# Macaron block (MoE, attention, MoE) on one core: the columns of 14 groups of normalised rows come from DMA transposes instead of TensorE

## The reference

```python
x = x + 0.5 * moe(layernorm(x))      # 4096 tokens of width 256
x = x + attention(layernorm(x))      # 4 sequences of 1024, 16 query heads, 4 key/value heads, RoPE
x = x + 0.5 * moe(layernorm(x))
# moe: softmax router over 32 experts, top 8 kept up to a share of 0.8; every expert is
# computed for every token: silu(x @ gate) * (x @ up) @ down, weighed per token
```

## Time and profile before

| | |
|---|---|
| median of 3 runs | 2312.97 us (2312.69 to 2313.44) |
| the profiled execution | 2313.61 us |
| its span in the profile | 2311.8 us |
| PE busy | 2240.8 us (97%) |
| DVE / ACT / POOL busy | 1581.2 / 1242.3 / 1063.5 us |
| PE in the chain that ended last | 90% |

### The profile page before, as it was taken

The page is one execution under the profiler, slowest core; times in us unless marked ns, Lnnn a source line. Parts: engine busy times, 40 slices in busy tenths (PEclk is TensorE's granted clock), DMA queues, the critical chain, the costliest instruction groups (busy, mean ns, idle before and its releaser), DMA issues.

```text
span 2311.8 us, 48013 instructions
## 1 busy us (share of the span) xinstructions
PE 2240.8 (97%) x19280; PEld 1498.7 (65%) x19280; DVE 1581.2 (68%) x3138; ACT 1242.3 (54%) x1973; POOL 1063.5 (46%) x864
## 2 busy tenths in 40 slices
PE   2999999999999999999999999999999999999998
PEld 2888875555565565565556555665655655688887
DVE  7766579877877877877777876676777753454543
ACT  4433331666666666566666566666656666533332
POOL 1866653443443443443434434333433434465665
PEclk9999999999999999999999999999999999999999
DMA  5210121011101011100110111010010010011010
GB/s 214 74 39 24 39 57 30 17 28 31 30 17 50 20 37 25 30 23 20 44 30 22 25 32 31 11 41 14 19 42 11 15 36 10 21 29 30 19 39 19
DMA packets 111878, 77.78 MB, mean 34 GB/s; under 512 B 57508, under 2 KB 103844, under 8 KB 110888
## 3 DMA queue, kind: packets, MB, share of 16 engines
q1 hardware_dynamic: 111512, 74.69, 11.7%
q10 hardware_dynamic: 144, 0.03, 0.0%
HBM read 62.87 MB, written 11.80 MB: 32 GB/s over the span
## 4 chain that ended last, share of the span: by engine, by line
PE 90%; DVE 7%; issue 1%; POOL 1%; ACT 0%; DMA 0%; POOLq 0%; DVEq 0%; ACTq 0%
PE PS L1128 42%; PE PS L1146 21%; PE PS L1158 11%; PE PS L1191 11%; DVE arena L912 1%; PE PS L1170 1%; PE PS L1110 1%; PE PS L1087 1%; PE PS L1232 1%; DVE XN L792 1%; PE PS L1218 1%; DVE turned L875 0%; POOL arena L543 0%; DVE arena L889 0%; DVE arena L897 0%
## 5 line engine op out<-in xcount | busy, mean ns | idle before, releaser
L1128 PE MATMUL PS<-XT,WGU 128*128 128x256 f16 x9216 | 1116.1, 274 | 37.3 <-DVE WGU L758 20.8
L1128 PEld LDWEIGHTS PS<-XT,WGU 128*128 128x128 f16 x9216 | 875.8, 98 | 262.1 <-issue 133.0
L548 POOL TENSOR_TENSOR arena<-arena 128x512 f16<-128x512 f32 x384 | 450.3, 1173 | 1139.0 <-ACT arena L624 1138.9
L912 DVE TENSOR_REDUCE arena<-PS 128x1 f32<-128x512 f32 x1024 | 657.5, 684 | 344.8 <-PE PS L1158 342.3
L647 ACT ACTIVATE arena<-PS,fac 128x512 f32<-128x512 f32 x1024 | 646.2, 684 | 240.4 <-PE PS L1170 239.2
L617 ACT ACTIVATE arena<-PS,fac 128x512 f32<-128x512 f32 x384 | 263.9, 687 | 706.4 <-PE PS L1128 706.3
L1146 PE MATMUL PS<-WD,arena 128*128 128x256 f16 x4608 | 569.2, 273 | 6.7 <-DVE X L904 4.7
L1146 PEld LDWEIGHTS PS<-WD,arena 128*128 128x128 f16 x4608 | 431.7, 98 | 149.5 <-issue 91.5
L543 POOL TENSOR_TENSOR arena<-arena 128x512 f32<-128x512 f32 x384 | 501.1, 1305 | 45.8 <-DVE arena L897 36.6
L889 DVE SCALAR_TENSOR_TENSOR arena<-arena,PS 128x512 f32<-128x512 f32 x384 | 260.9, 679 | 270.9 <-ACT arena L617 270.0
L1158 PE MATMUL PS<-arena 48*128 48x512 f16 x1024 | 312.6, 382 | 3.3 <-DVE arena L912 2.4
(11 more groups left out here) (116 smaller groups left out, 793.1 us busy)
## 6 DMA issues: line engine op xcount, KB each, us to landing
arena<-ce_scratch SPq DMA_DIRECT2D x256, 128.0 KB, 3.2
arena<-wgu SPq DMA_DIRECT2D x4, 1536.0 KB, 13.0
arena<-q_scratch SPq DMA_DIRECT2D x192, 32.0 KB
arena<-ktab_c SPq DMA_DIRECT2D x16, 256.0 KB, 4.0
q_scratch<-arena SPq DMA_DIRECT2D x32, 128.0 KB, 1.7
out<-X SPq DMA_DIRECT2D x8, 512.0 KB, 3.0
X<-wd SPq DMA_DIRECT2D x2, 1536.0 KB, 23.0
X<-x SPq DMA_DIRECT2D x1, 3072.0 KB, 11.4
```

Of the source, the lines that this page charges most:

```text
L548: pool.tensor_tensor(hs[1][:, d % HS, :], tw[d % 2], hs[0][:, d % HS, :], ALU.subtract).then_inc(lo_done, 1)
L912: dve.tensor_reduce(mx[:, half * REP * QT + c:half * REP * QT + c + 1], PS[:, B_MAX + half, :], AX_X, ALU.max).then_inc(max_taken, 1)
L1128: ins = pe.matmul(PS[:, b, j * HALF_G:(j + 1) * HALF_G], WGU[w][:, kt, part * CHUNKS + c + j, :], XT[r][:, k % 2, kt, half * HALF_G:(half ...
```

## The change

For every group turn but 0 and 3 (`BY_PE`), thus for 14 groups, `XT` is filled by DMA transposes from SP instead of by PE and ACT. `turn_rows(k + 1)` stands in SP's program at slot 14 of turn k, behind that slot's `spread`. It waits until the place in `XT` is free, waits for `xs_hi`, issues four transposes of 128 partitions x 256 elements (64 KB each) into `XT[0]`, waits for `xs_lo`, and issues four more into `XT[1]`. They count up `cols_in[0]` and `cols_in[1]`; `logits` waits for both. The events `t_hi` and `t_lo` of these groups, with their transposes on PE and copies on ACT, are gone. The next writers of `XS` (`rows_high`, `rows_low`) wait for the DMAs instead of the transposes. The norms of the projections and of groups 0 and 3 stay on PE and count their semaphores by `turn_on_pe`.

```diff
+BY_PE = (0, 3)
...
             for s, name in ((T_HI, "t_hi"), (T_LO, "t_lo"), (T_LOGITS, "logits")):
-                at[k * PER_GROUP + s].append((name, k + 1, 0))
+                if name == "logits" or k + 1 in BY_PE:
+                    at[k * PER_GROUP + s].append((name, k + 1, 0))
...
+            def turn_rows(k):
+
+                if 2 <= k <= GROUPS + 1:
+                    sp.wait_ge(j_done, JOINS * (k - 1))
+                if k > GROUPS + 1:
+                    sp.wait_ge(u_done, (k - 1) * PER_GROUP)
+                for h in range(2):
+                    sp.wait_ge((xs_hi, xs_lo)[h], norm_of_group(k) + 1)
+                    for t in range(GT):
+                        sp.dma_start_transpose(XT[h][:, k % 2, :, t * P:(t + 1) * P], XS[h][:, t, :])\
+                          .then_inc(cols_in[h], 16)
...
+                if s == 14 and 0 <= k < PREPS - 1 and k + 1 in BY_DMA:
+                    turn_rows(k + 1)
...
             def rows_low(i):
 
                 pool.wait_ge(xs_hi, i + 1)
+                if group_of_norm(i - 1) in BY_DMA:
+                    pool.wait_ge(cols_in[1], 64 * turn_by_dma(group_of_norm(i - 1)))
...
             def rows_high(i):
 
                 act.wait_ge(xn_ready, i + 1)
-                if i:
-                    act.wait_ge(t_lo, i)
+                if i and group_of_norm(i - 1) in BY_DMA:
+                    act.wait_ge(cols_in[0], 64 * turn_by_dma(group_of_norm(i - 1)))
+                elif i:
+                    act.wait_ge(t_lo, turn_on_pe(i - 1) + 1)
...
             def logits(k, bank):
-                pe.wait_ge(xt_lo, norm_of_group(k) + 1)
+                if k in BY_DMA:
+                    for h in range(2):
+                        pe.wait_ge(cols_in[h], 64 * turn_by_dma(k))
+                else:
+                    pe.wait_ge(xt_lo, turn_on_pe(norm_of_group(k)) + 1)
```

More of the change, by code:

```diff
@@ L166, in norm_of_join, with group_of_norm, turn_on_pe, turn_by_dma @@
     return 2 * g + 2
+def group_of_norm(i):
+    return i if i < 2 else (i + 1) // 2 if i % 2 and i <= 2 * GROUPS + 1 else i - GROUPS if i > 2 * GROUPS + 1 else None
+ON_PE = [i for i in range(PREPS + GROUPS) if group_of_norm(i) is None or group_of_norm(i) in BY_PE]
+BY_DMA = [k for k in range(PREPS) if k not in BY_PE]
+def turn_on_pe(i):
+    return ON_PE.index(i)
+def turn_by_dma(k):
+    return BY_DMA.index(k) + 1
 def build(nc, x, wgu, wd, wg, wq, wk, wv, wo, ident_c, ktab_c, kneg_c, out):
@@ L313, in build @@
                                                   sem("xt_lo"))
-        dve_link = sem("dve_link")
+        dve_link, cols_in = sem("dve_link"), [sem(f"cols_in{h}") for h in range(2)]
         logits_done, diff_ready, exp_ready = sem("logits_done"), sem("diff_ready"), sem("exp_ready")
@@ L597, in rows_high @@
                 act.wait_ge(xn_ready, i + 1)
-                if i:
-                    act.wait_ge(t_lo, i)
+                if i and group_of_norm(i - 1) in BY_DMA:
+                    act.wait_ge(cols_in[0], 64 * turn_by_dma(group_of_norm(i - 1)))
+                elif i:
+                    act.wait_ge(t_lo, turn_on_pe(i - 1) + 1)
                 act.activation(flat(XS[0]), flat(XN), ACT.Copy).then_inc(xs_hi, 1)
             def take_rows(i, slot, h, bank):
-                act.wait_ge((t_hi, t_lo)[h], i + 1)
+                act.wait_ge((t_hi, t_lo)[h], turn_on_pe(i) + 1)
                 act.activation(XT[h][:, slot, :, :].rearrange("p k n -> p (k n)"), bank16(bank), ACT.Copy)\
@@ L1104, in join @@
                     pe.wait_ge(small_split, 1)
-                pe.wait_ge(xt_lo, norm_of_join(g) + 1)
+                pe.wait_ge(xt_lo, turn_on_pe(norm_of_join(g)) + 1)
                 slot = g % 2
@@ L1254, in event @@
                     transpose_rows(turn, h, bank)
-                    taken[bank] = ((xt_hi, xt_lo)[h], turn + 1)
+                    taken[bank] = ((xt_hi, xt_lo)[h], turn_on_pe(turn) + 1)
                 if name in ("t_hi", "t_lo"):
```

## The result

| | before | changed |
|---|---|---|
| median | 2313.08 us (2312.69 to 2314.36, 6 runs) | 2299.81 us (2298.48 to 2303.14, 6 runs) |
| ratio, 95% interval | | 0.9943 (0.9931 to 0.9956) |
| profiled execution, span | 2313.61 / 2311.8 us | 2300.86 / 2298.9 us |

Beside the experiments the changed kernel was timed once more, at 2298.81 us, ratio 0.9936 (0.9923 to 0.9950). Of the five executions of one experiment's kernel, the one with one transpose per half, one took 3721.07 us at a mean granted clock of 0.561, which stays unexplained, and its ratio is that of the other four. The forecast was 2300.4 us. The change saves 13.3 us by the first comparison of medians, 0.57%; the interval of the ratio spans 10 to 16 us.

A forecast was written before the change was run, and what follows sets the result against it. PE's instruction stream was taken to bound the kernel: 2312.97 us, less 12.6 us for 28 transpose sets, plus 0 for DMA waits and queues, gives 2300.4 us (-0.54%). Own range 2297 to 2304 us; with rival 1, 2297 to 2326.

The forecast's parts named there:

- PE bounds the kernel: Whole kernel: PE, busy 2240.8 of 2311.8 us, sets the time; microseconds taken out count unless PE then waits.
- A set is worth 0.445 to 0.45 us: Eight transposes on PE: 0.445 us in quiet slots, 0.45 in the attention; 28 sets removed save 12.6 us.
- t of 0.6 to 1.3 us: SP's queue: what one DMA transpose adds, by the slower of SP's issue and the DMA engines; bounded by 0.32 and 5.0.
- my whole-row price: DMA engines: 64 KB moved in 256-byte rows, 256 packets, take 0.6 us per transpose.
- The threshold of 1.8 us per transpose: Logits of slot 17, quiet groups: PE begins to wait once t exceeds 1.8 us; in the attention, 3.3 us.
- 16.2 us of room: Group 1: from its high half being ready at 106.28 to PE reaching the logits at 122.5.
- The queues cost nothing: SP's program behind the transposes: stores, rows(1) and loads held up at no cost; group 3 stays on PE.
- Rival 1: Slow transposes, t = 2.37: PE waits at slot 17 in four quiet groups, 16.9 us, 2317.3 or 2324 us; 17%.
- Rival 1's price for the clock: Behind each of four quiet-group waits at the logits, a lowered clock costs 1.7 us, 6.9 us in all.
- Rival 2: Very slow transposes, t = 5.0 by 32-byte pieces, 2048 packets: waits in all groups, 237 us, 2537 us; 13%.
- Rival 3: Attention: PE reaches joins or projections earlier and waits for DVE, half of 9 us lost, 2305 us; 13%.
- The clock as noise: Start of a half turn: a 2.33 us PE wait may or may not bring 1.7 us of lowered clock.

The follow-up runs named there:

- Experiment 1: Changed kernel with PE doing its 28 transpose sets again, unread, and ACT's 28 copies still gone: 2313.43 us, ratio 1.0002 to the kernel before.
- experiments 2 and 6: experiment 2, and two kernels with one transpose per half: group 3 by DMA between the loads, 2297.95 us; projections by DMA too, 2290.63 us.
- experiment 2: Changed kernel with groups 1, 2, 14 and 15 back on PE, only attention groups 4 to 13 by DMA: 2303.65 us, ratio 0.9960.
- experiment 4: Changed kernel with plain 64 KB DMAs ahead of each group's transposes in SP's queue: sixteen 2320.25 us, eight 2300.72 us.
- experiment 5: Changed kernel with the same data in sixteen 32 KB transposes per group, 2327.92 us, or in one 256 KB transpose per half, 2298.89 us.

## Why the prediction was right, point by point

- **PE bounds the kernel.** Held. Experiment 1 puts the sets back and the time with them; experiments 2 and 6 find 0.46 to 0.49 us per set in the attention and at the projections by the times, and the marks of experiment 2 find 0.48.
- **A set is worth 0.445 to 0.45 us, read from start to start.** Held: 28 sets are 12.6 us; the medians say 13.3 and, beside the experiments, 14.8, with intervals that both take in 12.6, and the two marks in the trace are 13.1 us closer together. The group's 30.2 us of busy time for 384 transposes would have given 17.6 us.
- **t of 0.6 to 1.3 us.** Held in the median, at its upper end; in the mean of a group's eight, 1.40 us, it was just above, and below the 1.8 us that decides. That it came so near was partly luck. I had added 0.6 us of queue work to 0.43 us of issue. The trace has 1.25 us of issue and some 0.3 us of work of the DMA engines beside it; the issue of a transpose is more than twice that of a plain DMA of 64 KB from the same tile into DRAM (8.88 / 16 = 0.56 us in experiment 4). Landing was 2.4 us against my 2. Why one of the eight often takes 2 us or more is open.
- **The threshold of 1.8 us per transpose, and 16.2 us of room.** Held: 4 us of delay cost nothing that could be told, 9 us cost waits in the four quiet groups and nowhere else.
- **The queues cost nothing.** Held for the 14 groups: PE's waits in the trace after have none for a DMA. But one reading in it was wrong. I let rows(1), issued at 485.02, be untouched for t up to 2.5 us; the eight start at 468.81 and store_block with its 2.16 us (from 476.09 in the trace of before) stands in between, so the bound is (485.02 - 468.81 - 2.16) / 8 = 1.8 us. The measured t stayed below that too. Group 3 shows what it would have cost where the queue behind slot 14 is not idle. SP's queue in turn 3, after:

```profile
467.31 10.26 SPq L424 DMA_TRANSPOSE XT<-XS  x8
...
483.44 1.73 SPq L492 DMA_DIRECT2D m_scratch<-arena  x4
```

- **Rival 1** did not come, but experiment 5 shows how near it was: about ten or eleven instructions per group fill the room of the quiet groups, (16.2 - 2.4) / 1.40 or / 1.25, and the change has eight. The Trainium skill ("VectorE: DVE Perf Modes", The three transpose paths) lists 1309 ns for a 128 x 128 transpose by DMA. That lies near the 1.23 us that one takes here to issue on SP, and far from the 2.4 us until it has landed. Taking it twice for 128 x 256 was wrong: the issue doesn't grow with the size. The Trainium skill ("Advanced Engine Details and Errata", X-Bar Transpose (TRN2)) also says that transposing DMAs are as fast as regular ones. Here a transpose of 64 KB keeps the DMA engines busy for no longer than my whole-row price (0.33 against 0.6 us) and lands in 2.4 us where a plain store of 64 KB lands in 2.0, but its issue takes more than twice as long.
- **Rival 1's price for the clock was too low.** I took 1.7 us from a wait of 2.33 us; behind the two waits of over 4 us of experiment 4 it was 2.5 and 2.4 us. Behind the three waits of about 6 us of experiment 5 it was 2.4, 1.0 and 1.1 us, so it is not a fixed price either, and what sets it is open.
- **Rival 2** is refuted: a transpose has 288 packets and not 2048.
- **Rival 3** is refuted by the marks of experiment 2: 9.5 us less over the attention's 20 sets. PE's waits for DVE at projections are the same as in the earlier trace rows, and PE in a turn of the attention is busy for 165.91 of 168.00 us. The waits, and the table by stretches, after:

```profile
PE PS L1173 <- DVE turned L918: 8.3, 14, 1.2
```

```profile
1163.00:1331.00 168.00, 165.91 (x1405) 98.94 (x1402) 129.34 (x259) 104.77 (x170) 71.51 (x58) 1.00 0.13 32
```

- **The clock as noise.** The 2.33 us waits at the start of two half turns are still there. Before, the one near 310 us was followed by a lowered clock; after, it is the one near 206 us, and the other isn't:

```profile
208.21 2.74 PE L1191 MATMUL PS<-WD,arena 128*128 128x256 f16 x12 [2.33 <-DVE X L945]
210.74 3.08 PE L1173 MATMUL PS<-XT,WGU 128*128 128x256 f16 x24
...
312.15 1.48 PE L1191 MATMUL PS<-WD,arena 128*128 128x256 f16 x12 [2.34 <-DVE X L945]
```

The same wait costs 1.6 us of clock in one execution and none in another: the trace of experiment 4 with sixteen plain DMAs has a lowered clock behind both waits, those with eight plain DMAs ahead and with one transpose per half behind neither. A term of that size on either side of a comparison is no effect of the change.

## What to carry to other kernels

Where PE sets the time, a piece of work taken from it is worth the distance between starts with and without it, not its busy time, and it is won only if what replaces it is there before PE arrives: so count the room from the operand's readiness to PE's arrival in the tightest stage, and compare it with the number of instructions in the issuing queue. A queue that issues in order has to be read on past the new work; group 3 lost 12 us to save 0.9. For DMA transposes, fewer and larger ones are better, up to the 256 KB tried here: lay the source out so that one instruction covers it.

## What the runs showed of the hardware that I had not expected

- Issuing a DMA transpose out of SBUF takes SP 1.23, 1.25 and 1.28 us for 32, 64 and 256 KB in the median, with single ones up to 2.5 us; landing takes 2.4, 2.4 and 3.2 us from the start of the issue. A plain DMA of 64 KB from the same tile into DRAM takes 0.56 us to issue.
- A DMA transpose of 128 x 128, 128 x 256 or 128 x 1024 float16 elements makes 160, 288 or 1056 packets: one for each 256 bytes, and 32 more.
- 112 DMA transposes of 64 KB run beside a full PE stream without slowing it: with all sets kept on PE the ratio is 1.0002 (0.9993 to 1.0011), and two marks in the trace are 2167.68 us apart against 2167.66.
- A wait of PE of 4.2 us costs 2.5 us more, by a granted clock of 0.50 behind it, and one of 9.28 us 2.6 us more; three waits of about 6 us cost 1.0 to 2.4 us more, and waits of 2.33 us cost 1.6 to 1.7 us more in some executions and nothing in others.
